# A graph layer's first stage in another order: whole-tile loads, counts ahead of the fourth tile's products, and the jump between the last tile's halves

## The reference, cut to what matters

```python
def _sage_layer(h, edge_src, edge_dst, deg_inv, W_self, W_neigh, b):
    msg = h[edge_src]
    agg = jax.ops.segment_sum(msg, edge_dst, num_segments=h.shape[0])
    mean = agg * deg_inv[:, None]
    return h @ W_self + mean @ W_neigh + b
...
h = jax.nn.relu(_sage_layer(x, edge_src, edge_dst, deg_inv, W_self0, W_neigh0, b0))
out = _sage_layer(h, edge_src, edge_dst, deg_inv, W_self1, W_neigh1, b1)
...
x = x + _L0_gnn_ref(_layernorm(x, axis=-1), src, dst, ...)
x = x + _L0_ffn_ref(_layernorm(x, axis=-1)[None], ...)[0]
```

## Time and profile before

| what | value |
|---|---|
| median of 3 runs | 1278.19 us (1276.9 to 1279.23) |
| profiled execution: its own time | 1276.36 us |
| profiled execution: span from first to last instruction | 1274.6 us |
| TensorE (PE) busy | 1183.6 us, 93% of the span |
| VectorE (DVE), ScalarE (ACT), GpSimd (POOL) busy | 197.4, 87.2, 41.7 us |
| mean granted TensorE clock | 0.952 of full speed |

### The profile page before, as it was taken

The page is one execution under the profiler, slowest core; times in us unless marked ns, Lnnn a source line. Parts: engine busy times, 40 slices in busy tenths (PEclk is TensorE's granted clock), DMA queues, the critical chain, the costliest instruction groups (busy, mean ns, idle before and its releaser), DMA issues.

```text
span 1274.6 us, 10958 instructions
## 1 busy us (share of the span) xinstructions
PE 1183.6 (93%) x4448; PEld 666.9 (52%) x4448; DVE 197.4 (15%) x600; ACT 87.2 (7%) x175; POOL 41.7 (3%) x42
## 2 busy tenths in 40 slices
PE   6896999999999987799998999999997999999995
PEld 3452677644444553335344555444534994797442
DVE  7744000010122243200010000100001000000000
ACT  0111000000000010001000000000101000000000
POOL 0000000000000001000010000001010000000000
PEclk9998899999999995599998999999998999999998
DMA  6603000422001025363399223214969843645321
GB/s 214 268 1 126 10 1 1 132 97 68 17 16 33 17 94 204 104 251 158 110 364 405 85 116 132 100 25 124 385 221 407 359 189 117 218 158 206 108 110 21
DMA packets 38771, 183.83 MB, mean 144 GB/s; under 512 B 5593, under 2 KB 5593, under 8 KB 27338
## 3 DMA queue, kind: packets, MB, share of 16 engines
q1 hardware_dynamic: 34196, 168.25, 34.0%
q0 software_dynamic: 3776, 13.70, 4.3%
q10 hardware_dynamic: 630, 0.02, 0.0%
HBM read 170.51 MB, written 11.43 MB: 143 GB/s over the span
## 4 chain that ended last, share of the span: by engine, by line
PE 46%; issue 3%; ACT 1%; DVE 1%; POOL 0%; ACTq 0%; DVEq 0%; POOLq 0%
PE p_gu L511 27%; PE p_down L1112 16%; PE p_gu L1049 3%; PE p_xg L552 1%; DVE ys L467 0%; ACT xg L479 0%; ACT ht L479 0%; PE p_ht L1039 0%; PE p_ht L1084 0%; POOL out_dram L994 0%; ACT ht L484 0%; PE p_gu L552 0%; DVE ht L471 0%; ACTq L676 0%; DVEq L268 0%
## 5 line engine op out<-in xcount | busy, mean ns | idle before, releaser
L511 PE MATMUL p_gu<-xg,wg 128*128 128x224 f32 (+1 forms) x1056 | 265.1, 414 | 3.5 <-ACT xg L479 3.5
L511 PEld LDWEIGHTS p_gu<-xg,wg 128*128 128x128 f32 x1056 | 202.1, 192 | 65.9 <-issue 61.2
L1112 PE MATMUL p_down<-wd,ht 128*128 128x512 f32 (+1 forms) x616 | 230.0, 594 | 6.5 <-ACT ht L479 3.3
L1112 PEld LDWEIGHTS p_down<-wd,ht 128*128 128x128 f32 (+1 forms) x616 | 95.0, 175 | 132.6 <-issue 123.0
L511 PE MATMUL p_gu<-wg,xg 128*128 128x512 f32 (+1 forms) x288 | 117.0, 566 | 3.1 <-DVE ys L467 1.8
L511 PEld LDWEIGHTS p_gu<-wg,xg 128*128 128x128 f32 x288 | 54.9, 193 | 63.8 <-issue 56.7
L471 DVE TENSOR_TENSOR ht<-ht,p_gu 128x256 f32<-128x256 f32 (+3 forms) x63 | 27.5, 437 | 391.0 <-PE p_gu L511 243.3
L503 PE MATMUL p_y<-wn,h0T 128*125 128x512 f32 x160 | 74.1, 618 | 3.4 <-issue 2.9
L503 PE MATMUL p_h<-h0T,ws 128*128 128x313 f32 (+1 forms) x256 | 70.9, 439 | 5.9 <-ACT ok L479 5.9
L503 PE MATMUL p_sage<-ws,h1T 128*125 128x512 f32 x160 | 70.5, 593 | 0.0
L503 PE MATMUL p_y<-wn,h1T 128*125 128x512 f32 x160 | 68.8, 592 | 0.0
(11 more groups left out here) (149 smaller groups left out, 573.4 us busy)
## 6 DMA issues: line engine op xcount, KB each, us to landing
wg<-in_w_gu_dram SPq DMA_DIRECT2D x88, 1024.0 KB, 9.3
wd<-in_w_down_dram SPq DMA_DIRECT2D x88, 512.0 KB, 14.0
wn<-in_w_gnn_dram SPq DMA_DIRECT2D x16, 512.0 KB, 11.5
ws<-in_w_gnn_dram SPq DMA_DIRECT2D x16, 512.0 KB, 8.2
xa<-in_x_dram SPq DMA_DIRECT2D x5, 448.0 KB, 3.3
xr<-in_x_dram SPq DMA_DIRECT2D x5, 448.0 KB, 3.3
xfw<-xf SPq DMA_DIRECT2D x5, 448.0 KB, 3.1
out_dram<-xr SPq DMA_DIRECT2D x5, 448.0 KB, 3.1
```

The source lines that it names most:

```text
L511: got = h.matmul(o if m is None else o[:, :m], a, b if m is None else b[:, :m], start=n == 0, stop=n == len(pairs) - 1, skip_group_check=True)
L1112: got = h.matmul(o[job], *pairs[job][n], start=n == 0, stop=n == FC - 1, skip_group_check=True)
```

## The change

- `op(..., dma=n)`: an operation can hold n transfers. `load_rows` and `store_rows` become one operation of two transfers each, where they were two operations.
- `vector` and `plan` are written anew: tile 0's norm comes after 4 columns of edges (before: 9), `ln` 1 after 20 (before: 26). The products `y00` come after 4 counts (before: 14). All counts end ahead of `t3`; the plan ends with `y30`.
- NOH goes from 13 to 17 buffers; `vi` and `dig` move to the place beside the edge lists, and `deg_inv` from slot 24 to slot 26.
- `y31` is recorded behind the cutting of the digits. `normal` 4, `tr(4)` and `y40` come after the comparison `ok_i` and ahead of the reading of the register. `y41` comes behind the jump.
- Banks: the degree sums take banks 0 and 1 and `p_most` bank 2; after the jump the order of banks begins with 5.

```diff
     def load_rows(to, of):
-        for lo, hi in ROWS:
-            load(to[lo:hi], of[lo:hi])
+        def fn(h, s):
+            for lo, hi in ROWS:
+                h.dma_start(to[lo:hi], of[lo:hi]).then_inc(s, 16)
+        return k.op("SP", fn, w=[to], dma=len(ROWS))
...
-    NOH = 13
+    NOH = 17
...
-    vector = [("rows", c) for c in range(9)] + [("ln", 0)] + [("rows", c) for c in range(9, 26)] + [("ln", 1)]
-    vector += [("rows", c) for c in range(26, 38)] + [("normal", 2)] + [("rows", c) for c in range(38, 70)]
-    vector += [("normal", 3)] + [("rows", c) for c in range(70, EC)] + [("normal", 4)]
+    vector = [("rows", c) for c in range(4)] + [("ln", 0)] + [("rows", c) for c in range(4, 20)] + [("ln", 1)]
+    vector += [("rows", c) for c in range(20, 37)] + [("normal", 2)] + [("rows", c) for c in range(37, 71)]
+    vector += [("normal", 3)] + [("rows", c) for c in range(71, EC)] + [("normal", 4)]
...
-    plan = [*range(14), "t0", "y00", *range(14, 20), "y01", *range(20, 26), "t1", "y10", *range(26, 38), "y11",
-            *range(38, 51), "t2", "y20", *range(51, 64), "y21", *range(64, 77), "t3", "y30", *range(77, EC), "t4", "y31"]
+    plan = [*range(4), "t0", "y00", *range(4, 20), "y01", "t1", "y10", *range(20, 37), "y11", *range(37, 54), "t2", "y20",
+            *range(54, 71), "y21", *range(71, EC), "t3", "y30"]
...
     for g in range(NDIG):
         ts(dig[g % 2], vi, 3 * g, 7, ALU.logical_shift_right, ALU.bitwise_and)
         copy(c16[:, :, g * DIG:(g + 1) * DIG], dig[g % 2], "ACT")
+    rows_times(y0, 3, 1, h0T, wn0, "p_y")
...
     ts(ok_i, ok[:, 0:1], float(EDGES), None, ALU.is_equal)
+    advance(("normal", NT - 1))
+    tr(NT - 1)
+    rows_times(y0, NT - 1, 0, h0T, wn0, "p_y")
     for eng in ("PE", "ACT", "DVE"):
         read_reg(eng, body, (eng, "count"), ok_i, 1)
     bodies = {(eng, "count"): [(1, None), (0, None)] for eng in ("PE", "ACT", "DVE")}
     hint("count", bodies)
-    rows_times(y0, 4, 0, h0T, wn0, "p_y")
-    rows_times(y0, 4, 1, h0T, wn0, "p_y")
     scaled(c16[:, :, :N])
...
     k.close()
-    ring[:] = range(8)
+    ring[:] = [5, 6, 7, 0, 1, 2, 3, 4]
+    rows_times(y0, NT - 1, 1, h0T, wn0, "p_y")
```

More of the change, by code:

```diff
@@ L256, in emit @@
             if o["dma"]:
-                used[lane] = [used[lane][0] + 16, i]
+                used[lane] = [used[lane][0] + 16 * o["dma"], i]
                 o["mark"], o["lane"] = (("D", lane), used[lane][0]), lane
@@ L365, in gnn_moe @@
     p = space(slot(24), slot(32))
-    vi = p("vi", [TP, NT, DIG], I32)
-    dig = [p(f"dig{i}", [TP, NT, DIG], I32) for i in range(2)]
     hrow = [p(f"hrow{i}", [TP, D]) for i in range(2)]
-    NOH = 13
+    NOH = 17
     onehot = [(p(f"os{i}", [TP, NT, PART], HP), p(f"od{i}", [TP, DIG + 1], BF)) for i in range(NOH)]
-    deg_inv = sb("deg_inv", [TP, N], FP, slot(24))
+    deg_inv = sb("deg_inv", [TP, N], FP, slot(26))
     wn0, ws0, wn1, ws1 = (sb(n, [128, KD, D], FP, slot(8 * i)) for i, n in enumerate(("wn0", "ws0", "wn1", "ws1")))
@@ L381, in gnn_moe @@
     node_f = p("node_f", [TP, NT, PART])
+    vi = p("vi", [TP, NT, DIG], I32)
+    dig = [p(f"dig{i}", [TP, NT, DIG], I32) for i in range(2)]
     xa = sb("xa", [TP, NT, D], FP, R4)
@@ L454, in load_rows, with fn @@
     def load_rows(to, of):
-        for lo, hi in ROWS:
-            load(to[lo:hi], of[lo:hi])
+        def fn(h, s):
+            for lo, hi in ROWS:
+                h.dma_start(to[lo:hi], of[lo:hi]).then_inc(s, 16)
+        return k.op("SP", fn, w=[to], dma=len(ROWS))
     def store_rows(to, of):
-        return [store(to[lo:hi], of[lo:hi]) for lo, hi in ROWS]
+        def fn(h, s):
+            for lo, hi in ROWS:
+                h.dma_start(to[lo:hi], of[lo:hi]).then_inc(s, 16)
+        return k.op("SP", fn, r=[of], dma=len(ROWS))
     def load_gu(e, c):
@@ L652, in gnn_moe @@
             rows_times(y0, int(w[1]), int(w[2]), h0T, wn0, "p_y")
-    assert not vector
     memset(const_ones, 1.0)
@@ L680, in degrees @@
         for i, (n0, nn) in enumerate(HALVES):
-            q = any_bank("p_deg")[:TP]
+            q = bank("p_deg", i)[:TP]
             mm(q[:, :nn], [(one, of[:, s, n0:n0 + nn]) for s in range(NT)])
@@ L691, in gnn_moe @@
         reduce_max(ok[:, i:i + 1], q[0:1, :nn], ALU.add)
-    q = any_bank("p_most")[:TP, :1]
+    q = bank("p_most", 2)[:TP, :1]
     mm(q, [(const_ones, most16)])
@@ L738, in gnn_moe @@
     k.cls = 0
-    mm(any_bank("p_most")[:TP, :1], [(const_ones, most16)])
+    mm(bank("p_most", 2)[:TP, :1], [(const_ones, most16)])
     copy(ok[:, 1:2], ok[:, 0:1])
@@ L818, in gnn_moe @@
         layernorm(xf[t % 2], xr[:, t, :], t)
-        xf_stores += store_rows(xfw[t * TP:(t + 1) * TP, :D], xf[t % 2])
+        xf_stores.append(store_rows(xfw[t * TP:(t + 1) * TP, :D], xf[t % 2]))
         if t:
@@ L968, in gnn_moe @@
             stt(o, q, wt[:, t, NE:], o, ALU.mult, ALU.add)
-        out_stores += store_rows(out[t * TP:(t + 1) * TP, :], xr[:, t, :])
+        out_stores.append(store_rows(out[t * TP:(t + 1) * TP, :], xr[:, t, :]))
     for j in range(3, NTL):
```

## The result

The changed kernel takes 1260.49 us (median of 4 runs, 1259.31 to 1264.67) against 1277.55 us for the kernel before on the same chip (median of 4, 1275.99 to 1279.23). The ratio of the means is 0.9872, with a 95% interval of 0.9846 to 0.9898, which is 13 to 20 us. By the medians it is 17.1 us faster, where 18.3 us and a time of 1259.9 us were forecast. The profiled execution took 1259.31 us, with a span of 1257.4 us.

What follows compares the result with a forecast made beforehand. TensorE is busy 93% of the span, so only its idle or lower-clock time can be won. `p_h` beginning at 114.55 instead of 129.54 us, plus 3.3 us, gives 18.3 us: 1259.9 from median 1278.19, range 1257 to 1264.

Steps and rivals of the forecast that it cites:

- The beginning: First stage up to the end of `y30`: one-operation loads and new order end it at 81.1 us, 8.7 us earlier.
- the slower rival: At the start: the early burst of loads starves `wn0`, `y00` can't end before 41 us; 1280 to 1281 us, chance 0.05.
- My 20 us: Loads at the start: tile 0, `wn0` and tiles 1 to 4 are in by about 20 us, at 411 GB/s.
- the rival in which the change of order brings nothing: At the start: tiles 1 to 4 still late, up to 8.7 us less gained, 1264 to 1269 us; chance 0.06.
- The digits: Cutting of digits after `y30`: 5.7 us, from 81.1 to 86.8, hidden while TensorE makes `y31` until 88.05.
- the 0.9: At `y40`: allowance for a start at the lower clock, taken between 0 and 1.8 us.
- The jump: Between `y40` and `y41`: ScalarE's 5.85 us wait goes; `y41` begins at 104.9 us, TensorE idles 4.6 us.
- the rival with 1266.4 us: At the jump: the register reading waits until TensorE has drained; 11.8 us gained, chance 0.18.
- the other rival (1254): At the jump: both of TensorE's jumps fit under `y40`, `y41` ends at 107.8 us; chance 0.17.
- the 8.3 us of the earlier trace: Price of TensorE's two jumps, taken from another exit and entry, 668.08 to 676.38 us, in the kernel before.
- The clock behind the gap: At `y41`, after TensorE's idle time: 1.8 us lost to the lower clock, up to 3.3.
- `p_h`'s warm start: First products of `p_h`: run at full clock, saving the 3.3 us lost before.

Runs made afterwards that it cites:

- the split: The changed kernel with each tile's load again as two operations; not run, so no measured time.
- the load alone: The kernel before with each tile's load as one operation and nothing else changed; not run, so no measured time.

## Why the prediction was right, step by step

The time lay 0.6 us from the forecast. That is partly luck. Several terms were off by 1 to 2 us, in both directions. And the gain of 17.1 us is 1.2 below the 18.3 that was forecast: the time was counted from a median of 1278.19, and the median of the kernel before is now 1277.55.

**The beginning: right in kind, 1.7 us short.** `y00` began at 13.49 us (forecast 12.8, before 18.74), and took 9.37 us. A half at full clock has a row of 7.13, so the loss was 2.2 where I had 1.25 for the clock; and the transposition ahead of it took 1.8 us up to `y00` where I had 1.28. Two things could make such rows, the lower clock or weights that land late (the slower rival). The loading of weights into TensorE under `y00` tells them apart. First one of the slow part, then one behind it, then one behind the gap at the jump, where the granted clock reads 0.73:

```profile
14.50 0.33 PEld L508 LDWEIGHTS p_y<-wn,h0T 128*125 128x125 f32 x1 [0.52 <-issue]
...
18.83 0.19 PEld L508 LDWEIGHTS p_y<-wn,h0T 128*125 128x125 f32 x1 [0.24 <-issue]
...
108.20 0.33 PEld L508 LDWEIGHTS p_y<-wn,h0T 128*125 128x125 f32 x1 [0.52 <-issue]
```

The instruction itself is 0.33 us long in place of 0.19, and the steps between two of them are 0.85 us up to 17.9 and 0.43 us from 18.4 on. Length, idle time and step are those of the stretch with the low granted clock (0.33, 0.52 and 0.85 us there). So this is the lower clock, though the granted clock reads 1.00 here; and with no wait of TensorE for a load, nothing shows that the burst starved `wn0`.

**The tiles of x landed later than I reckoned.** My 20 us took 411 GB/s for all of it. VectorE's moments still waited for `xa` four times, 2.6 us in all, and the second tile was normalised at 31.74 in place of 29.1. TensorE came to it at 32.50, so the slack was 0.8 us and not 1.8, but the wait of the earlier trace rows is gone as forecast, and with it the rival in which the change of order brings nothing. Stretches of the changed kernel (columns as in the earlier trace rows) show what the rate was:

```profile
8.00:12.00 4.00, 0.27 (x2) 0.28 (x3) 3.51 (x18) 0.00 (x0) 0.00 (x0) 1.00 1.03 416
12.00:16.00 4.00, 4.00 (x11) 2.42 (x11) 4.00 (x17) 1.16 (x2) 0.00 (x0) 1.00 1.04 398
16.00:20.00 4.00, 4.00 (x8) 1.66 (x7) 3.78 (x16) 0.00 (x0) 0.00 (x0) 1.00 1.03 238
20.00:24.00 4.00, 4.00 (x44) 2.34 (x43) 2.97 (x6) 0.59 (x1) 0.00 (x0) 1.00 1.05 248
```

In the 8 us in which the moments of tiles 1 and 2 waited, the DMA engines were as busy as before (1.03, 1.05) but moved 238 and 248 GB/s. This is the term that was mis-sized. The moments of the first and the last of these four tiles began, behind their waits, at

```profile
20.41 1.29 DVE L524 BATCH_NORM_STATS2 ln_st<-xa 125x6 f32<-125x512 f32 x2 [0.63 <-DMA xa<-in_x_dram]
...
26.96 1.29 DVE L524 BATCH_NORM_STATS2 ln_st<-xa 125x6 f32<-125x512 f32 x2 [0.69 <-DMA xa<-in_x_dram]
```

which is a tile of 0.51 MB every 2.18 us, or 235 GB/s: about all that the DMA engines moved from 16 to 24 us. So the slow stretch is the one in which they served the tiles of x, one behind another. Why they were slower than the weights is not shown.

What part of the gain is the loads' and what part the new order's is not shown either: that needed the split and the load alone. The two traces allow an estimate. VectorE's waits for `xa`, before and after, in total, times, longest:

```profile
DVE ln_st L519 <- DMA xa<-in_x_dram: 7.2, 4, 2.1
DVE ln_st L524 <- DMA xa<-in_x_dram: 2.6, 4, 0.7
```

Without its 7.2 us, the kernel before would have had the second tile's row at about 32.0 in place of 39.2, and TensorE came for it at 35.2 (39.3 less the wait of 4.1). With them, the changed kernel would have it at 39.2 at the earliest, and TensorE came at 32.5. So by this estimate the old loads would have kept TensorE waiting in the new order too, some 6.7 us, and the new loads alone would have ended the old wait.

**The digits: right.** `y30` ended at 82.8 (forecast 81.1; the 1.7 us are those of the beginning). Its copy to the last cast took 5.66 us, as in the earlier trace rows, under the second half, with 1.0 us to spare. The degree sums, warm, and the comparison took from 89.69 to 92.74, 3.05 us (forecast 3.1; 5.1 in the earlier trace rows). TensorE stood still for 2.32 us behind `p_most`, while VectorE made the comparison and then the last tile's row (forecast 2.3). The half behind it started at the full clock: 7.13 us, so the 0.9 that I had put in as a middle between 0 and 1.8 was 0.

**The jump: the size right, its parts not as I had them.** The register and branch instructions of TensorE's sequencer, in the stretch from 85 to 145 us of the changed kernel: line, instruction, count, nanoseconds (shortest, median, longest), first and last start.

```profile
L672 PEldq TENSOR_LOAD <-ok_i x1: 493/493/493, 95.3 to 95.3; - x1
L680 PEldq BRANCH_PREFETCH_HINT  x1: 53/53/53, 96.7 to 96.7; - x1
L289 PEldq COMPARE_BRANCH  x2: 4060/4412/4765, 97.0 to 101.3; - x2
L289 PEldq BRANCH_PREFETCH_HINT  x1: 36/36/36, 101.2 to 101.2; - x1
```

The reading begins at 95.3, half a microsecond after the start of `y40` and 6.5 us before its end. So TensorE's queue need not drain for it here, and the rival with 1266.4 us is out. The two branches fill the rest: the one into the body starts at 97.0 and takes 4.06 us, the one out of it starts at 101.3 and takes 4.77, up to 106.07. `y41` begins at 106.10. From `y40`'s start to `y41`'s it is 11.27 us; I had 11.6, within its bounds of 10.4 to 12.8. Only 7 of it lies under `y40`, and so the entry is hidden and most of the exit is not. That disposes of the other rival (1254), in which both are.

The Trainium skill (Advanced Engine Details and Errata, Control Flow Timing) gives 51 and 108 ns for branches. The branches in the row above take 4060 and 4765 ns, so for TensorE the measurement decides; ScalarE's two are recorded with 43 and 61 ns, near those figures, but 3.2 us pass from the first of them (103.3) to its copy in the body (106.47). The Trainium skill (Runtime: NRT & Kernel Launch, Instruction fetch mechanics) puts a stall on taken branches to code that is not at hand; the long branches agree with that, but no run here shows that fetching is what they wait for.

One term of the forecast rested on a nearby row that was not taken apart: the 8.3 us of the earlier trace rows stood for leaving one body and entering the next. The branches of TensorE there, in the kernel before, and at another change of experts:

```profile
L289 PEldq COMPARE_BRANCH  x2: 299/3536/6773, 668.2 to 669.3; - x2
...
L289 PEldq COMPARE_BRANCH  x2: 285/1240/2195, 934.0 to 935.2; - x2
```

Leaving took 0.30 us, and entering 6.77. At all seven changes of experts leaving took 0.29 to 0.33 us, and entering 2.1 to 6.8, at each place within 0.5 us of the same in both kernels (6.62 and 2.36 at these two in the changed kernel). The row that I took is the longest of the seven. In the jump of the first stage both branches are long, 8.8 us together. So the sum held partly by luck, and the split did not hold.

**The clock behind the gap: right.** `y41` took from 106.10 to 114.77, 8.67 us (forecast 8.75), and `p_h` ran warm. The granted clock there:

```profile
104.00:108.00 4.00, 1.90 (x3) 0.81 (x4) 0.84 (x4) 0.19 (x1) 0.00 (x0) 0.85 0.73 255
108.00:112.00 4.00, 4.00 (x8) 1.74 (x7) 0.00 (x0) 0.00 (x0) 0.00 (x0) 0.73 1.00 384
112.00:116.00 4.00, 4.00 (x12) 2.06 (x11) 0.00 (x0) 0.59 (x1) 0.00 (x0) 1.00 0.20 81
```

**What lies behind keeps the gain.** The first product of the table of places, `p_pos`, starts at 444.37 us in place of 462.12: 17.75 us earlier, what `p_h` had gained. The waits of TensorE at the experts are the same to 0.3 us each. At the scaled outputs `ys` the lead is 17.87 us at first (598.92 for 616.79), 19.35 in the middle (802.39 for 821.74) and 17.17 at the last (1244.10 for 1261.27). So up to 1.5 us come and 2.2 us go there. Where they do, the granted clock differs: from 662.25 to 682.25 us it is 0.98 in the changed kernel, and 0.88 in the same work of the kernel before (680 to 700); from 1062.25 to 1082.25 it is 0.91 for 1.00 (1080 to 1100). Why it does was not followed further.

The sum, by its terms: up to the end of the fourth tile's first half 7.0 us were gained (forecast 8.7); from there to the start of `p_h` 7.8 (forecast 6.3; of the 1.5 more, 0.9 is the clock at `y40` that was not paid, 0.3 the jump, 0.1 `y41`, and 0.2 the way to `y40`); and 3.0 by `p_h`'s warm start (forecast 3.3). Together that is 17.7 in place of 18.3; a term that was too large and one that was too small nearly cancel.

## What to carry to other kernels

A jump on a runtime value cost each engine that took part several microseconds here (on TensorE 9.1 us, from 97.0 to 106.07), going in or coming out, and what covered them was work already in that engine's queue. So look for the engine that stands at a wait of its own when it comes to the jump (here ScalarE), give TensorE products that don't depend on it, and count both branches against the queued time. One branch of TensorE took 0.3 to 6.9 us in these traces, so its price is read at its own place. Work of a slow chain between two other engines (here the digits) belongs under products that were going to run anyway. And where a helper tracks dependences coarsely, two transfers that don't overlap can still wait for each other; a trace of the issuing queue's waits shows it.

## What the runs showed of the hardware that was not expected

- The granted clock of a stretch read 1.00 from 12 to 16 us, while products and weight loads in it ran at half the pace (0.85 us from load to load, against 0.43). Here the pace is the better witness.
- The way out of a body of a single product took TensorE 4.77 us here. In the kernel before, the same branch is 6.86 us long and cost nothing, because `y41` was still running until then; how much of that length is waiting for the products is not shown:

```profile
L289 PEldq COMPARE_BRANCH  x2: 358/3608/6857, 116.1 to 116.6; - x2
```

- In that row the way in took 0.36 us, where the prefetch hint for the jump stood 8.2 us ahead of the branch (107.9 and 116.1). In the changed kernel the hint stood 0.3 us ahead, and the way in took 4.06. The lead of the hint alone doesn't explain this. At the first expert it is about 9 us in both kernels (525.0 to 534.0 before, 507.4 to 516.3 after), and the way in took 0.40 us before and 4.83 after:

```profile
L289 PEldq COMPARE_BRANCH  x1: 403/403/403, 534.0 to 534.0; - x1
...
L289 PEldq COMPARE_BRANCH  x1: 4831/4831/4831, 516.3 to 516.3; - x1
```

- ScalarE's branch records are short, and its time lies behind them. From the branch into the body to the copy in it, 5.4 us pass in the kernel before (123.9 to 129.30), with the hint 16 us ahead, and 3.2 us in the changed kernel (103.3 to 106.47), with the hint just ahead. Before and after:

```profile
L289 ACTq COMPARE_BRANCH  x2: 43/52/61, 123.9 to 129.3; - x2
...
L289 ACTq COMPARE_BRANCH  x2: 43/52/61, 103.3 to 106.5; - x2
```

- The DMA engines were fully busy at 416 GB/s and, eight microseconds later, when the tiles of x came, at 238. Why was not found.
